# Tile 1's sources on a load semaphore of their own, and VectorE's scores and one-hots of tile 0 ahead of the edge records

## The reference

```python
a = h[src] @ Ws.T + h[dst] @ Wd.T + emb_rel[etype] @ Wr.T
e = leaky_relu((a @ attn_fc2_w.T)[:, 0], 0.01)
m = segment_max(e, dst); w = exp(e - m[dst])
alpha = w / segment_sum(w, dst)[dst]
agg = segment_sum(alpha[:, None] * h[src], dst)
x = layernorm(x + where(deg > 0, agg, h) + h @ loop_weight)
# then two layers: h = rrelu(segment_sum((rel[etype] + h[src]) @ W_r, dst) * norm + self)
x = layernorm(x + h)
```

## Time and profile before

| | us |
|---|---|
| median of 3 runs (all: 2779.62, 2778.87, 2776.01) | 2778.87 |
| the profiled execution, its own time | 2776.1 |
| its span | 2774.0 |
| PE busy | 2149.1 (77%) |
| DVE busy | 2045.1 (74%) |
| POOL busy | 1591.4 (57%) |
| ACT busy | 1223.8 (44%) |

### The profile page before, as it was taken

One profiled execution on the slowest core, in us unless ns is written; L12 is line 12 of the kernel. 1 busy time (PEld: TensorE's weight loads), 2 busy tenths in 40 slices (PEclk: granted clock), 3 DMA queues, 4 the chain that ended last, 5 costly groups with the idle time before them and its releaser, 6 DMA issues.

```text
span 2774.0 us, 45483 instructions
## 1 busy us (share of the span) xinstructions
PE 2149.1 (77%) x16208; PEld 1802.6 (65%) x16208; DVE 2045.1 (74%) x4582; ACT 1223.8 (44%) x3215; POOL 1591.4 (57%) x1672
## 2 busy tenths in 40 slices
PE   1366676667767777777787788788787999999998
PEld 0255565556666666666676676676675876888887
DVE  5889998887888888888888888888797456333333
ACT  1255665555556456555555555555555323000000
POOL 6767777777777777777777777777774000000000
PEclk9988887888888988888889888999899999999999
DMA  8545554554555554554555555555454354666664
GB/s 219 145 126 173 173 153 153 157 165 152 160 175 151 156 181 146 159 183 148 160 186 151 160 190 153 168 183 156 148 177 152 112 156 133 215 211 211 217 211 158
DMA packets 184632, 463.50 MB, mean 167 GB/s; under 512 B 86336, under 2 KB 113784, under 8 KB 164577
## 3 DMA queue, kind: packets, MB, share of 16 engines
q1 hardware_dynamic: 116050, 339.10, 36.4%
q0 software_dynamic: 53600, 114.17, 16.4%
q10 hardware_dynamic: 14752, 7.26, 1.0%
HBM read 362.54 MB, written 97.84 MB: 166 GB/s over the span
## 4 chain that ended last, share of the span: by engine, by line
POOL 50%; PE 25%; issue 17%; DVE 6%; DMA 1%; ACT 1%; SPq 1%; ACTq 0%; POOLq 0%; DVEq 0%
POOL arena L559 50%; PE pair L951 19%; DVE arena L1114 2%; PE bank L875 1%; PE pair L924 1%; PE bank L836 1%; PE pair L954 1%; DMA wlp<-n_L_gnn_loop_weight_dram 1%; DVE arena L1084 1%; PE pair L805 1%; PE pair L782 0%; DMA group_starts<-endv 0%; SPq L434 0%; DVE arena L1194 0%; DVE arena L1092 0%
## 5 line engine op out<-in xcount | busy, mean ns | idle before, releaser
L559 POOL DMA_INDIRECT arena<-rows,srcw x1617 | 1541.6, 953 | 518.8 <-issue 491.4
L1114 DVE TENSOR_TENSOR arena<-bank,idx 128x2000 bf16<-128x2000 bf16 (+3 forms) x700 | 560.4, 853 | 21.1 <-PE pair L805 17.9
L951 PE MATMUL pair<-arena 125*125 125x384 bf16 x3285 | 551.4, 326 | 1.6 <-DVE arena L1316 1.6
L805 PE MATMUL pair<-arena 128*128 128x250 bf16 x2500 | 348.9, 287 | 260.0 <-DVE arena L1114 206.5
L581 ACT ACTIVATE arena<-pair 99x264 f32<-99x264 f32 (+2 forms) x410 | 279.0, 712 | 593.8 <-PE pair L805 448.5
L951 PEld LDWEIGHTS pair<-arena 125*125 125x125 bf16 x3285 | 447.4, 136 | 103.3 <-issue 8.4
L675 ACT ACTIVATE arena<-arena,wexp 128x128 f32<-128x128 bf16 x1650 | 487.4, 387 | 1.6
L875 PE MATMUL bank<-arena 128*125 128x130 f32 x3300 | 485.2, 318 | 0.0
L875 PEld LDWEIGHTS bank<-arena 128*125 128x125 f32 x3300 | 474.6, 230 | 4.2
L805 PEld LDWEIGHTS pair<-arena 128*128 128x128 bf16 x2500 | 239.7, 102 | 339.4 <-DVE arena L1114 267.0
L1084 DVE TENSOR_TENSOR arena<-arena,bank 128x4224 bf16<-128x4224 int16 x150 | 344.2, 2350 | 1.7
(11 more groups left out here) (250 smaller groups left out, 2312.6 us busy)
## 6 DMA issues: line engine op xcount, KB each, us to landing
arena<-counts SPq DMA_DIRECT2D x106, 812.5 KB, 4.4
counts<-arena SPq DMA_DIRECT2D x50, 1562.5 KB
arena<-dst SPq DMA_DIRECT2D x50, 1056.0 KB
arena<-etype SPq DMA_DIRECT2D x50, 1056.0 KB
arena<-rows,srcw POOLq DMA_INDIRECT x1617
arena<-counts SPq DMA_DIRECT2D x14, 281.2 KB, 2.8
edge_terms<-arena SPq DMA_DIRECT2D x200, 12.4 KB
xt<-in_x_dram SPq DMA_DIRECT2D x50, 62.5 KB
```

The costliest lines, as they stand in the source:

```text
L559: pool.indirect_dma_start(out=rows[:, q, c, :], out_offset=None, in_=rows0, in_offset=bass.IndirectOffsetOnAxis(ap=srcw[:, q, c:c + 1], ax ...
L805: r = pe.matmul(group_of(n, gi), ohl[:, sl, gi * GC + c, :], ohm[:, sl, gi * GC + c, :], start=(c == 0), stop=(c == GC - 1))
L951: r = pe.matmul(o, ring[0:TN, m % RD, h - h0, :], hs[k][0:TN, h, :], start=(h == first), stop=(h == last - 1))
L1114: return v.tensor_tensor(hot_.rearrange("p c (j t) -> p c j t", t=2), iotap[:, 0:w].rearrange("p (j t) -> p j t", t=2)[:, None, :, :].broa ...
```

## The change

Three things. First, the sources of a tile get a load semaphore of their own (`ld_s0`, `ld_s1`), and POOL waits for that one instead of for all three lists. Second, in SP's start the order is: tile 1's sources, tile 0's two broadcasts, tile 0's lists and `xt`, tile 1's lists and `xt`, the padding store, tile 1's broadcasts. Third, VectorE runs `first_scores()` at the very start of `dve_fast`, ahead of the weight block, and `records()` after `prepare_edges(0)`. POOL's wait for the lists of tile 2 moves behind the ten record gathers.

```diff
         def sp_fast(sp):
+            def load_sources(t, first):
+                sp.dma_start(srcw[:, t % 2, :], src[bass.ds(first, WIN)].rearrange("(p c) -> p c", c=C)).then_inc(s("ld_s%d" % (t % 2)), 16)
...
+            f1 = window(1)
+            load_sources(1, f1)
+            f0 = window(0)
+            sp.wait_ge(s("st_l16"), 64)
+            load_wide(0, f0)
+            load_lists(0, f0)
+            load_lists(1, f1)
             sp.wait_ge(s("pad_ready"), 1)
             sp.dma_start(rec[E // GRAN:E // GRAN + 6], agg2[0:6, 0, 0:2 * GRAN]).then_inc(s("st_rec"), 16)
-            f0 = load_lists(0)
-            sp.wait_ge(s("st_l16"), 64)
-            load_wide(0, f0)
-            f1 = load_lists(1)
             load_wide(1, f1)
...
             for t in range(1, NT):
                 q = t % 2
-                pool.wait_ge(s("ld_w%d" % q), 48 * (t // 2 + 1) - (0 if q else 16))
                 if t == 2:
                     pool.wait_ge(s("st_rec"), 48)
...
+                pool.wait_ge(s("ld_s%d" % q), 16 * (t // 2 + q))
                 if t >= 2:
                     pool.wait_ge(s("acc_c"), NAC * (t - 1))
...
         def dve_fast(v, link):
...
+            first_scores()
             for k in range(2):
                 v.wait_ge(s("relW_ps"), k + 1)
...
-            records()
             v.wait_ge(s("st_rows"), ROWS_STORED)
             prepare_wide(0)
-            first_scores()
             prepare_edges(0)
+            records()
             terms(0)
```

More of the change, by code:

```diff
@@ L439, in sp_fast, with window, load_lists @@
         def sp_fast(sp):
-            def load_lists(t):
-                first = sp.value_load(plan_i[0:1, t:t + 1], min_val=0, max_val=E - WIN)
+            def load_sources(t, first):
+                sp.dma_start(srcw[:, t % 2, :], src[bass.ds(first, WIN)].rearrange("(p c) -> p c", c=C)).then_inc(s("ld_s%d" % (t % 2)), 16)
+            def window(t):
+                return sp.value_load(plan_i[0:1, t:t + 1], min_val=0, max_val=E - WIN)
+            def load_lists(t, first):
                 if t >= 2:
                     sp.wait_ge(s("u_done"), t - 1)
-                for a, w in ((src, srcw), (dst, dstw), (etype, etw)):
-                    if t >= 1 or a is not src:
-                        sp.dma_start(w[:, t % 2, :], a[bass.ds(first, WIN)].rearrange("(p c) -> p c", c=C)).then_inc(s("ld_w%d" % (t % 2)), 16)
+                if t >= 2:
+                    load_sources(t, first)
+                for a, w in ((dst, dstw), (etype, etw)):
+                    sp.dma_start(w[:, t % 2, :], a[bass.ds(first, WIN)].rearrange("(p c) -> p c", c=C)).then_inc(s("ld_w%d" % (t % 2)), 16)
                 sp.dma_start(xt[0:TN, t % 3, :], x[t * TN:(t + 1) * TN]).then_inc(s("ld_xt%d" % (t % 3)), 16)
-                return first
             def load_wide(t, first):
@@ L506, in sp_fast @@
                 if t + 2 < NT:
-                    f2 = load_lists(t + 2)
+                    f2 = window(t + 2)
+                    load_lists(t + 2, f2)
                     load_wide(t + 2, f2)
@@ L1057, in dve_fast, with first_scores @@
         def dve_fast(v, link):
+            def first_scores():
+                v.wait_ge(s("gath_x"), 16 * C)
+                for c0, c1 in ((0, XP), (XP, C)):
+                    w = c1 - c0
+                    link(v.tensor_tensor(prod[:, 0:w, :], rows[:, 0, c0:c1, 0:D], vb[:, None, 0:D].broadcast_to([P, w, D]), ALU.mult))
+                    link(v.tensor_reduce(rows[:, 0, c0:c1, D], prod[:, 0:w, :], AX, ALU.add))
+            first_scores()
             for k in range(2):
@@ L1085, in matches @@
                                        two[:, None, :].broadcast_to(shape), ALU.is_equal)
[L1087 to L1092, removed]
             def prepare_wide(t):
@@ L1119, in prepare_edges @@
                 q = t % 2
-                v.wait_ge(s("ld_w%d" % q), 48 * (t // 2 + 1) - (0 if q else 16))
+                v.wait_ge(s("ld_w%d" % q), 32 * (t // 2 + 1))
                 v.tensor_scalar(dl2[:], dstw[:, q, :][:, :, None].broadcast_to([P, C, 2]), thr[:, t:t + 1], None, ALU.subtract)
```

## The result

Over 14 runs of each, the changed kernel took 2771.34 us (2769.43 to 2774.05) and the kernel before 2777.65 us (2775.89 to 2779.62). The ratio is 0.9977, 95% interval 0.9970 to 0.9984: 6.3 us faster, by the interval 4.4 to 8.3. The forecast was 5.7 us, and 2773.2 us for the median. It started from the median of three runs, 2778.87 us; over 14 runs the kernel before is 1.2 us faster than that, which is most of the 1.9 us between 2773.2 and 2771.34. The profiled execution has a span of 2770.1 us.

A forecast was written before the change was run, and what follows sets the result against it. VectorE's chain up to tile 1's sum bounds the start of tile 3's gathers, then POOL sets the pace. 1.95 + 3.8 = 5.75, say 5.7 us: 2778.9 - 5.7 = 2773.2 us, range 2768 to 2778.5.

The forecast's parts named there:

- VectorE's chain sets the start of tile 3, and POOL carries it to the end: Tile 3's gathers wait for tile 1's sum, behind VectorE; their start, 177.9 instead of 183.65 us, shifts the end one to one.
- POOL's half is worth nothing: Tile 1's gathers start about 8 us earlier, at about 59, but gain 0, since POOL waits at tile 3 anyway.
- Scores and weight block, 1.95 us: VectorE's front: scores 59.3 to 68.85, weight block from 69.7 once PE has xt; 1.95 us won, bounds 2.8 and -2.9.
- The order of the queue: SP's loads: xt pays for broadcasts ahead of it; if small loads could pass, the gain would be 6.6 instead of 5.7.
- the last rival: Slower: xt stuck behind the broadcasts; gain eaten if it lands at 72.9, 2781.9 us if at 76; chance 0.06.
- The wait behind types_in(0), 3.8 us: At L1154, VectorE's wait for PE shrinks because PE's 33 matmuls run beside the records; 3.8 us won, bounds 3.0 and 4.4.
- lower bound of 3.0: Smallest gain at VectorE's L1154 wait for PE, 3.0 us, if PE runs the pair at half clock.
- drw: no cost: terms(0) reads drw without waiting: 21 us lie between `hotT_ready` and the read, against 16.4 before; cost 0.
- PE colder in the sums: Rival: idle PE regains its full clock later in the sum, losing 1.5 us; 2776.2 with later xt; chance 0.22 including later xt.
- The chances: Forecast 0.45, colder PE or later xt 0.22, more won 0.20, no effect 0.07, slower 0.06.
- more won: Rival: gathers and xt land 3 to 4 us sooner, weight block at 66; gain 9.4 us, 2769.5 us; chance 0.20.
- the weak cases: Outcomes placed within 0.2%: colder PE or somewhat later xt, chance 0.22, and no effect, 2778.9 us, chance 0.07.

The follow-up runs named there:

- VectorE's half alone: Kernel before, with only `first_scores()` moved to the head of `dve_fast` and `records()` behind `prepare_edges(0)`; SP and POOL untouched: 2770.03 us, ratio 0.9973.
- SP's half alone: Changed kernel with VectorE back in its old order, keeping SP's new load order and POOL's own load semaphore: 2783.93 us, ratio 1.0023 against the kernel before.
- the run of the scores alone: Kernel before, with only `first_scores()` moved to the front; records stay ahead of `prepare_wide(0)`, SP and POOL as before: 2781.44 us, ratio 1.0013.

## Why the prediction was right

- *VectorE's chain sets the start of tile 3, and POOL carries it to the end.* Right: 5.53 us at tile 3, 6.47 at the last gather, 6.3 in the medians. POOL's wait in front of tile 3 remained. That the terms come out at 5.2 us up to the second answer of PE, and the medians at 6.3, is agreement within the scatter.
- *POOL's half is worth nothing.* Right: VectorE's half alone is 7.7 us faster, so the other half adds nothing to it that can be seen. Alone that other half is 6.2 us slower, which is xt's place on the queue and not the head start. Tile 1 started at 60.87 rather than 59, and the records landed by 115.44, within the 114 to 117 that I called likely.
- *Scores and weight block, 1.95 us.* It was 2.20 at terms(0), but for another reason than I gave, so the size of this term is right by luck. xt landed by 65.41, not 67.2, so PE had the product ready in time (in SP's half alone, with xt at 65.42, the weight block starts at 67.94) and the scores' end decided: the weight block at 69.48 (forecast 69.7, released by PE). Two errors offset each other: xt 1.8 us too late, and the scores' start 0.6 too early (59.3 against 59.91). The run of SP's half alone, where nothing covers xt, pays for its place.
- *The order of the queue.* xt came 5.8 us later than before, but 3.4 of these are its later issue (58.66 against 55.27), behind SP's issues of the broadcasts. From issue to use it took 6.75 us against 4.31. The 2.4 us more agree with broadcasts that are served first; no run here separates that from a queue that is busier in general. That the queue was full before, as the last rival has it from the longer issues, is not shown either: the broadcasts' issues took 1.18 and 2.29 us after, and xt was still far from the 72.9 at which the gain is eaten.
- *The wait behind types_in(0), 3.8 us.* 3.40 at the first answer, for PE is at its lower clock there (granted 0.50; 0.59 us for the pair L870 instead of 0.38), and 0.4 more is lost at the second answer, which I had not counted. The forecast took the pair at the old clock, though its own lower bound of 3.0 had the case.
- *drw: no cost.* Right for the changed kernel, but I did not see that this cover is a condition of the whole: without the records in that place the wait for it is 8.86 us.
- *PE colder in the sums.* From cc to tile 0's sum it took 13.17 us after and 13.28 before, and the 66 products 10.37 and 10.49: no loss. In both, PE began the sum at a granted clock of 0.50 and ended it at 1.00.
- *The chances.* Half of the forecast's 0.45 and all of the 0.20 for "more won" are 0.425, not the 0.46 stated for a gain beyond 0.2%, and the other half with the weak cases is 0.515, not 0.49. The measured gain, 0.23% with an interval of 0.16 to 0.30%, does not settle on which side of 0.2% it lies.

## What to carry to other kernels

Follow one clock from the end back to where the stream that sets the pace last waited for somebody; an edit is worth what it moves that point, and a head start of the stream itself is worth nothing while it still waits there. Before moving a piece of work out of its place, ask what it hid: a DMA round trip of 16 us lay under the scores and one-hots with about 1 us to spare, and only moving other work into the same place kept the move from being a loss. And an idle gap is best filled by what can be ready at its beginning: 8 us of weights, not scores that have to wait for its end.

## What the runs showed of the hardware

- PE's lower granted clock costs a small, steady amount on a short visit: the f32 pair took 0.58 or 0.59 us and VectorE's wait for it was 1.02 us in all eight profiles (the other chip's left aside) in which that pair no longer stood behind the 33 matmuls, against 0.38 us for the pair in the kernel before. PE had been idle for 9.95 us in the changed kernel, and for only 3.90 us in the run of the scores alone, with a granted clock of 0.50 both times. An idle stretch alone does not tell the clock: in the kernel before, PE came out of 12.98 us of idle time in front of L782 at a granted clock of 1.00 (109.5 to 114.5 us).
- The landing of a gather went with the stores beside it and not with its own issue. The last x gather was issued at 50.6 to 51.4 us in all ten profiles on the faster chips. In the seven in which VectorE waited for it, the scores began the later the later SP had begun its stores of `rows0`, to within 0.3 us: stores at 39.82 us, scores at 58.42; 40.98, 59.91; 41.29, 59.63; 41.97, 60.60; 42.51, 61.41; 42.89, 61.28; 43.27, 61.38. Why was not tested.
- One more load of 62.5 KB among the first inputs went with scores at 61.28 to 61.41 us in three kernels out of three, against 58.42 to 60.60 in four profiles without it. That it is this load was not shown separately.
- The same kernel took 2777.73 and 2777.17 us on two chips and 4550.85 on a third, with waits of up to 42 us for which the profile names no releaser, and, in the four kernels run there, a mean granted clock of 0.74 instead of about 0.90. What the waits are stays open.
